# Layer 2 attention: two heads per multiply slot, each in its own 64 array rows, with the row maxima sent to the stacks by DMA

## The reference, cut to what matters

```python
q = (x @ Wq).reshape(b, t, N_HEADS, HEAD_DIM).transpose(0, 2, 1, 3)   # 32 heads of 16
k = (x @ Wk).reshape(b, t, N_KV, HEAD_DIM).transpose(0, 2, 1, 3)      # 8 heads of 16
...
q = _apply_rope(q, cos, sin)
k = _apply_rope(k, cos, sin)
k_h = jnp.repeat(k, GROUP_SIZE, axis=1)
v_h = jnp.repeat(v, GROUP_SIZE, axis=1)
scores = jnp.einsum('bhqd,bhkd->bhqk', q, k_h) / math.sqrt(HEAD_DIM)
scores = jnp.where(causal[None, None], jnp.finfo(scores.dtype).min, scores)
attn = jax.nn.softmax(scores, axis=-1)
ctx = jnp.einsum('bhqk,bhkd->bhqd', attn, v_h)
```

## Time and profile before

| | |
|---|---|
| median of 3 runs | 1157.61 us (1157.04 to 1157.73) |
| the profiled execution | 1157.12 us, with a span of 1155.6 us in the trace |
| busy: PE, PEld | 1124.1 us (97%), 935.9 us (81%) |
| busy: DVE, ACT, POOL | 742.3 us (64%), 649.1 us (56%), 471.3 us (41%) |
| mean granted TensorE clock | 0.997 of full speed |

### The profile page before, as it was taken

How to read it: one execution, slowest core, us unless ns; L and a number is a source line. 1 busy time by engine, 2 the same in 40 slices (tenths; PEclk the granted TensorE clock), 3 DMA queues, 4 the chain that set the end, 5 groups by cost and what they waited for, 6 DMA issues and landing times. The chain is left out here.

```text
span 1155.6 us, 19856 instructions
## 1 busy us (share of the span) xinstructions
PE 1124.1 (97%) x6378; PEld 935.9 (81%) x6378; DVE 742.3 (64%) x2399; ACT 649.1 (56%) x1492; POOL 471.3 (41%) x537
## 2 busy tenths in 40 slices
PE   7899999999999999999999999999999999999997
PEld 6788888888888888888888878888888777776786
DVE  6767776667776666776677782222334778887675
ACT  6656665566765666765666644544212366666524
POOL 4654553345554355544444333333203355354300
PEclk9999999999999999999999999999999999999999
DMA  6011110011110011100100002221200223421001
GB/s 234 19 37 38 37 37 28 23 37 38 37 37 28 22 45 30 46 29 19 37 28 1 28 19 57 81 73 45 66 1 19 63 59 79 127 61 32 2 1 73
DMA packets 30361, 51.20 MB, mean 44 GB/s; under 512 B 5680, under 2 KB 6576, under 8 KB 30256
## 3 DMA queue, kind: packets, MB, share of 16 engines
q1 hardware_dynamic: 29680, 48.85, 14.9%
q10 hardware_dynamic: 576, 1.05, 0.3%
HBM read 38.35 MB, written 2.10 MB: 35 GB/s over the span
## 5 line engine op out<-in xcount | busy, mean ns | idle before, releaser
L487 POOL TENSOR_TENSOR turned<-turned,sin 128x512 f32<-128x512 f32 x73 | 94.4, 1293 | 310.2 <-ACT turned L347 310.2
L1719 DVE CUSTOM_DVE_ANT_0 f_masked<-bank,a_mask 128x512 f32<-128x512 f32 (+3 forms) x256 | 110.0, 486 | 26.2 <-PE bank L1931 21.7
L363 ACT ACTIVATE probs<-probs,neg_max 128x256 f32<-128x256 f32 (+1 forms) x256 | 119.8, 473 | 11.3 <-DVE neg_max L580 11.3
L490 POOL TENSOR_TENSOR turned<-turned,by_cos 128x512 f32<-128x512 f32 x73 | 101.0, 1384 | 5.7
L96 PE MATMUL bank<-wo_hi,oT_hi 128*128 128x512 f32 x256 | 100.3, 392 | 1.6 <-DVE oT_lo L643 1.6
L734 PE MATMUL bank<-xT_hi,wq_hi 128*128 128x512 f32 x256 | 101.7, 397 | 0.0
L734 PE MATMUL bank<-xT_lo,wq_hi 128*128 128x512 f32 x256 | 100.3, 392 | 0.0
L734 PE MATMUL bank<-xT_hi,wq_lo 128*128 128x512 f32 x256 | 100.1, 391 | 0.0
L96 PE MATMUL bank<-wo_hi,oT_lo 128*128 128x512 f32 x256 | 99.9, 390 | 0.0
L96 PE MATMUL bank<-wo_lo,oT_hi 128*128 128x512 f32 x256 | 99.7, 389 | 0.0
L422 ACT ACTIVATE pT_hi<-bank 128x512 fp32r<-128x512 f32 x112 | 61.6, 595 | 52.0 <-PE bank L773 52.0
(11 more groups left out here) (247 smaller groups left out, 3213.5 us busy)
## 6 DMA issues: line engine op xcount, KB each, us to landing
staged<-weights SPq DMA_DIRECT2D x70, 256.0 KB, 2.7
f_staged<-weights_f SPq DMA_DIRECT2D x33, 256.0 KB, 2.7
f_q_stack<-a_qT_hi SPq DMA_DIRECT2D x64, 64.0 KB, 2.0
rows<-x_rows SPq DMA_DIRECT2D x2, 1024.0 KB, 7.2
f_k_stack<-a_kT_hi SPq DMA_DIRECT2D x64, 32.0 KB, 2.0
f_q_stack<-a_qT_lo SPq DMA_DIRECT2D x32, 64.0 KB, 2.0
out<-rows SPq DMA_DIRECT2D x8, 256.0 KB, 2.0
a_raw<-weights_qkv SPq DMA_DIRECT2D x4, 384.0 KB, 4.8
```

Source lines behind the costliest of these rows:

```text
L363: act.activation(probs[:, s % 2, h, 0:width], probs[:, s % 2, h, 0:width], ACT.Exp, bias=neg_max[:, s % 2, h:h + 1], scale=SCALE0, accum_o ...
L487: pool.tensor_tensor(at, at, sin[:, :], ALU.mult).then_inc(sin_done, 1)
L490: pool.tensor_tensor(at, at, by_cos_at(a, first), ALU.add).then_inc(roped, 1)
L1719: dve.tensor_tensor_reduce(masked[:, bank * SEQ + at:bank * SEQ + at + seen], ps_s[bank][:, at:at + seen], mask[:, SEQ - seen:SEQ], -1.0, ...
```

## The change

Keys and queries are laid out anew. Of the 64 rows of one half of the array, row 4d + part holds dimension d of a head's part (high, low, high), so one head's stack fills 64 rows, and two heads of a pair stand in the two halves. Each multiply names only its half's rows; `scores(j, piece)` and `cross(j, piece)` issue the pair's two multiplies of a tile one behind the other, into different banks. Every fourth row of the key stack holds ones; four rows of the query stack take the maxima of the pair. These arrive by DMA: ACT copies the turned maxima of a whole unit (eight rows) to `shift_rows`, and SP sends them on (`load_shift`, two DMAs per unit); since the scores are taken from the same stack before, SP first clears those rows (`clear_shift`).

The heads' pieces are now items: item 6j + 2*piece + n is head n of pair j. Three banks serve all items in turn, for scores and for cross alike, so two items of one piece take two banks. `ps_o` is one bank where it was two, and the eighth bank takes the turned maxima. `apply` has two parts. Keys are turned doubled, in four parts where there were two, so there are twelve turns; two of them (10 and 11) stand at pair 9. Key DMAs carry 32 rows where they carried 16, and there are four query and key stacks.

```diff
@@ -1193,7 +1193,8 @@
-STACK = PARTS * PAIR_ROWS
+HALF = P // 2
+SPREAD = HALF // HD1
...
+ITEMS = 2 * PIECES
 SCORES_AT = {3: (0, 0), 2: (1, 0), 0: (1, 3 * P), 1: (2, 0)}
+SCORE_TILES = ((3,), (2, 0), (1,))
+MAXIMA_AFTER = (1, 2, 4, 6, 7, 8)
+PAIR_MAXIMA = 2 * SEQ_TILES
...
-STACKS = 3
...
+STACKS = 4
...
-APPLY_KEYS = ((0,), (1,), (3, 2))
+APPLY_KEYS = ((0, 3), (1, 2))
...
-PARTS_IN_LOOP = {0: 7, 1: 8, 2: 9}
...
+TURNS = [("q", 0), ("q", 1), ("q", 2), ("q", 3), ("k", 0), ("k", 1), ("q", 4), ("q", 5), ("q", 6), ("q", 7), ("k", 2), ("k", 3)]
...
+PARTS_IN_LOOP = {(0, 2): 8, (1, 1): 9, (9, 1): 10, (9, 2): 11}
...
-        ps_s, ps_t, ps_o = psum[0:3], psum[3:6], psum[6:8]
+        ps_s, ps_t, ps_o, ps_max = psum[0:3], psum[3:6], psum[6], psum[7]
...
+        def before_items(n):
+            return PAIR_MAXIMA * (n // ITEMS) + (MAXIMA_AFTER[n % ITEMS - 1] if n % ITEMS else 0)
...
+                    sp.dma_start(k_stacks[u % STACKS][part::SPREAD, :].bitcast(F32),
...
+            def load_shift(u):
+                sp.wait_ge(max_in, u + 1)
+                for pair in range(2):
+                    sp.dma_start(q_stacks[u % STACKS][SHIFT_STEP - 1::SHIFT_STEP, pair, :].bitcast(F32),
+                                 shift_rows[PAIR_SHIFTS * pair:PAIR_SHIFTS * (pair + 1), u % 2, :].bitcast(F32)
+                                 ).then_inc(shift_in, 16)
...
+            for u in range(STACKS - 1):
+                load_keys(u)
+                load_queries(u, 0)
+                load_queries(u, 1)
+            load_shift(0)
+            for u in range(STACKS - 1, UNITS1):
...
+                if u >= STACKS:
+                    sp.wait_ge(crossed, 2 * ITEMS * (u - STACKS + 1))
+                load_keys(u)
+                if u >= STACKS:
+                    clear_shift(u)
+                load_queries(u, 0)
+                load_shift(u - STACKS + 2)
+                load_queries(u, 1)
...
+                if j == 10:
+                    act.wait_ge(stack_in[(KV1 - 1) % STACK_SEMS][0], keys_in(KV1 - 1))
...
+            pool.memset(shift_places[:, :, :].bitcast(F32), 0.0)
+            for r in range(STACKS):
+                pool.memset(q_stacks[r][:, :, :].bitcast(F32), 0.0)
+                ones_in = pool.memset(k_stacks[r][:, :].bitcast(F32), 1.0)
...
+            def maxima(j, piece):
...
+                for n in range(2):
+                    item = ITEMS * j + 2 * piece + n
+                    dve.wait_ge(scored, item + 1)
+                    for qt in SCORE_TILES[piece]:
...
+                    if j % 2 == 0 and piece == 1 and u >= 2:
+                        join(u - 2)
+                    if j % 2 == 1 and piece == 2 and u >= 1:
+                        evacuate(u - 1)
+                    if j + AHEAD_PAIRS < PAIRS1:
+                        maxima(j + AHEAD_PAIRS, piece)
+            join(UNITS1 - 2)
...
+            def scores(j, piece):
+
+                u, pair = divmod(j, 2)
+                r = u % STACKS
+                if piece == 0:
+                    pe.wait_ge(stack_in[u % STACK_SEMS][pair], keys_in(u) if pair == 0 else 16 * PARTS * (u // STACK_SEMS + 1))
+                items = [ITEMS * j + 2 * piece + n for n in range(2)]
+                if items[1] >= 3:
+                    pe.wait_ge(max_done, before_items(items[1] - 2))
+                for qt in SCORE_TILES[piece]:
+                    at, seen = SCORES_AT[qt][1], (qt + 1) * P
+                    for n, item in enumerate(items):
+                        rows_at = slice(n * HALF, (n + 1) * HALF)
+                        mm = pe.matmul(ps_s[item % 3][:, at:at + seen], q_stacks[r][rows_at, pair, qt * P:(qt + 1) * P],
+                                       k_stacks[r][rows_at, 0:seen], start=True, stop=True, skip_group_check=True)
+                        if qt == SCORE_TILES[piece][-1]:
+                            mm.then_inc(scored, 1)
...
+            def cross(j, piece):
+
+                u, pair = divmod(j, 2)
+                r = u % STACKS
+                if j == 0 and piece == 0:
                     pe.wait_ge(part_lo, PARTS_AFTER[TILES - 2][0] + 1)
+                if pair == 0 and piece == 0:
+                    pe.wait_ge(shift_in, 16 * 2 * (u + 1))
+                items = [ITEMS * j + 2 * piece + n for n in range(2)]
+                if items[1] >= 3:
+                    pe.wait_ge(exp_done, items[1] - 2)
+                for kb in CROSS_KEYS[piece]:
+                    at = CROSS_AT[kb][1]
+                    for n, item in enumerate(items):
+                        rows_at = slice(n * HALF, (n + 1) * HALF)
+                        mm = pe.matmul(ps_t[item % 3][:, at:at + SEQ - kb * P], k_stacks[r][rows_at, kb * P:(kb + 1) * P],
+                                       q_stacks[r][rows_at, pair, kb * P:SEQ], start=True, stop=True, skip_group_check=True)
+                        if kb == CROSS_KEYS[piece][-1]:
+                            mm.then_inc(crossed, 1)
...
-                if u >= 2 and part == 0:
-                    pe.wait_ge(finished, u - 1)
+                if u >= 1 and part == 0:
+                    pe.wait_ge(finished, u)
...
+            scores(0, 2)
+            for piece in range(PIECES):
+                scores(1, piece)
+            scores(2, 0)
             turn_maxima(0)
+            scores(2, 1)
+            scores(2, 2)
+            for piece in range(PIECES):
+                scores(3, piece)
+            for j in range(PAIRS1):
+                u = j // 2
+                for piece in range(PIECES):
+                    cross(j, piece)
+                    if j + AHEAD_PAIRS < PAIRS1:
+                        scores(j + AHEAD_PAIRS, piece)
+                    if j % 2 == 0 and piece == 1 and u + 1 < UNITS1:
+                        turn_maxima(u + 1)
+                    if (j, piece) in PARTS_IN_LOOP:
+                        turn_part(PARTS_IN_LOOP[j, piece])
+                    if u >= 1 and (j % 2, piece) == (0, 2):
+                        apply(u - 1, 0)
+                    if u >= 1 and (j % 2, piece) == (1, 0):
+                        apply(u - 1, 1)
+                    if u >= 1 and (j % 2, piece) == (1, 2):
+                        turn_output(u - 1)
```

More of the change, by code:

```diff
@@ L1296, in attention1 @@
         o_tok = q_tok
[L1297 to L1300 removed]
+        k_stacks = [sb(f"k_stack{r}", [P, SEQ], F32R) for r in range(STACKS)]
         last_pT = sb("last_pT", [P, RING - FIRST_PT, HEAD_PROBS])
@@ L1471, in _ @@
                         sp.dma_start(place[:, :, :], w_f1[some].rearrange("k p c -> p k c")[:, :, 0:D]).then_inc(main_in, 16)
+            for u in range(UNITS1 - STACKS + 2, UNITS1):
+                load_shift(u)
             for tile in range(TILES):
@@ L1617, in turn_rows @@
                 pool.tensor_tensor(q_tok[:, tile, :], by_cos[:, 0:D], by_sin[:, 0:D], ALU.add).then_inc(tok_done, 1)
-                pool.tensor_tensor(k_tok[:, tile, :], by_cos[:, D:], by_sin[:, D:], ALU.add).then_inc(tok_done, 1)
+                turned = k_tok[tile // SEQ_TILES][:, tile % SEQ_TILES, :].rearrange("p (g a d) -> p g a d", a=2, d=HD1)
+                cos_part, sin_part = (by[:, D:].rearrange("p (g a d) -> p g a d", a=1, d=HD1).broadcast_to([P, KV1, 2, HD1])
+                                      for by in (by_cos, by_sin))
+                pool.tensor_tensor(turned, cos_part, sin_part, ALU.add).then_inc(tok_done, 1)
             for tile in range(TILES - 1):
@@ L1747, in _ @@
                     low_part(j)
-            maxima(0)
-            maxima(1)
+            for piece in range(PIECES):
+                maxima(0, piece)
             rotate(TILES - 1)
-            maxima(2)
-            maxima(3)
-            for s in range(SLOTS1 + 1):
-                if s in PARTS_IN_LOOP:
-                    low_part(PARTS_IN_LOOP[s])
-                if s % GROUP1 == 0 and s >= 2 * GROUP1:
-                    join(s // GROUP1 - 2)
-                if s % GROUP1 == 3 and s > GROUP1:
-                    evacuate(s // GROUP1 - 1)
-                if s + AHEAD_SCORES < SLOTS1:
-                    maxima(s + AHEAD_SCORES)
+            for j in range(1, AHEAD_PAIRS):
+                for piece in range(PIECES):
+                    maxima(j, piece)
+            for j in range(PAIRS1):
+                u = j // 2
+                for piece in range(PIECES):
+                    if (j, piece) in PARTS_IN_LOOP:
+                        low_part(PARTS_IN_LOOP[j, piece])
+                    if j % 2 == 0 and piece == 1 and u >= 2:
[5 more added lines that the diff above has]
+            join(UNITS1 - 2)
             steps = [0]
@@ L1908, in turn_part @@
                 else:
-                    pe.wait_ge(tok_done, 2 * (n + 1) * SEQ_TILES)
-                    pieces = [k_tok[:, n * SEQ_TILES + tile, :] for tile in range(SEQ_TILES)]
-                if j == 7:
-                    pe.wait_ge(sin_done, 4 * TILES)
-                elif j >= 8:
+                    b, c = divmod(n, 2)
```

(7 more changed lines are left out.)

271 lines of the change are left out of this document (100 added, 171 removed).

## The result

The changed kernel takes 1201.89 us (median of 4, 1200.94 to 1203.79) against 1157.55: slower by a ratio of 1.0386, 95% interval 1.0368 to 1.0404. I had forecast 1177.5 and a range up to 1196: the direction was right, but of the 44.3 us lost my sum had 20.4, less than half.

What follows compares the result with a forecast made beforehand. PE bound the kernel before, DVE next; after the change, their waits set the pace: 924.4 + 11.3 + 13 x 10.65 + 3.8 + 7.8 + 6.8 = 1092.6, 20.2 later; 20.4 put on 1157.12 gave 1177.5 us, range 1149 to 1196.

Steps and rivals of the forecast that it cites:

- The bound and the way it is reached: In the loop: PE's sum falls to 6.5 to 7 us per unit, under DVE's 7.8, but waits between engines set the pace.
- walk: One loop unit followed wait by wait from its first cross: next unit at 10.44 us, DVE idle 2.6, PE 3.
- My 0.2 on top: Per loop unit: 0.2 us added to the walk, as the kernel before walked 9.62 against 9.84 measured; gives 10.65.
- The clock: Longer start wait and PE's gaps in the loop may bring slow-clock stretches again, about 1 us each; not in the sum.
- The first cross: Way into the loop: first cross at 924.4, where before it was 914.14, behind the scores of four whole pairs.
- DVE's start at 909.1: Ahead of the loop: DVE starts the maxima near 909.1, 0.4 later for four more turnings of the second key part.
- My 1.2 for waits at pieces: Ahead of the first cross: about 1.2 us of DVE's waits at pieces, one term of the 924.2.
- The parts: Parts 10 and 11, at pair 9: two DVE waits for PE's turning and ACT's high part, 3.8 us in all.
- The halves: A pair's multiplies in the array's two row halves run at once, some ns apart; four groups of 0.65 per unit.
- The rival's unit of 11.65 + 0.2: Rival that the halves do not overlap, chance 0.10: loop unit 11.65 + 0.2 us, 19 us more, 1196 in all.
- DVE keeps full: Rival, chance 0.17: PE returns in time, loop unit is DVE's 7.85 us, total 1141; decides at 9.1 per unit.
- SP, POOL and the switches: SP's DMAs 7.6 of 10.65 us per unit and POOL's clearing cost nothing; row-group switches some 0.9 per unit.

Runs made afterwards that it cites:

- full_rows: Changed kernel with every multiply of scores and cross over all 128 rows, pairs serial, both heads summed, exponential of a ten-thousandth: 1201.09 us.
- fill: Changed kernel with three unread 512-column multiplies over all 128 rows added on PE per unit, units 1 to 13 save 4: 1194.94 us.
- copy_early: Changed kernel with DVE's copy of a unit's outputs moved alone, to the second pair's second piece: 1180.12 us.
- own_bank: Changed kernel with the sixth turned part (second key part) given bank 1 for itself: 1198.01 us.
- order: Changed kernel with only places moved: apply in three parts, maxima turned a piece later, DVE's copy and division a piece earlier: 1172.52 us.
- low_later: Changed kernel with scores ten pieces ahead, another order, second key part's own bank, unread multiplies added at the start, low parts a piece later: 1152.76 us.
- one_half: Changed kernel with both heads of a pair multiplying from rows 0 to 63, second head's own keys and queries left out: 1266.90 us.
- best_full_rows: low_later with serial pairs over all 128 rows, both heads summed, exponential of a ten-thousandth: 1163.84 us.

## Why the prediction failed, step by step

- **The bound and the way it is reached.** Right. PE's sum fell and the three shared banks, with PE in order, set the pace: walk 10.44, measured 10.49; DVE's idle time 2.6, measured 2.4; `turn_output`'s wait 1.07, measured 0.91. My 0.2 on top was not needed at full clock (13 x 0.16 = 2.1 too much).
- **The clock.** The step that failed: "may bring such stretches again, about 1 us each". I had named the cause and a price, and put no term in the sum, since I gave it no count. The price was near (0.6 to 2.2 us per unit); the count was twelve of thirteen units. Together that is some 16.5 in units 1 to 13 (what 10.49 and the parts leave), which full_rows confirms (0.9 left there, the clock full) and fill in part (7.0 won while work was added). The 2.7 at the end is the clock's as well: unit 14 took 10.5 with a stretch at 0.50 in it, and 7.7 in fill and 7.8 in copy_early at full clock, the forecast's 7.8. I misread the one row I had, 0.88 behind the loop's start: in the kernel before that is one fall, right behind a thin place (PE busy 1.09 of 2.00 us from 921 to 923), and PE then has no such gap again until the loop's end. The changed kernel has 2.3 us of waits in every unit, so the fall comes back again and again. "No gain can come from it" was right.
- **The first cross.** 931.2, not 924.4. DVE's start at 909.1 was the wrong term, by 4.9: I charged the second key part 0.4 for its turnings and did not look at the bank it goes to. PE's wait of 2.65 and the half clock behind it (0.83 in 895 to 905) made it 913.96; own_bank gave 3.9 back. My 1.2 for waits at pieces was 2.5 (0.47, 0.60, 0.59, 0.60 and 0.28 in DVE's timeline). The rest of the 6.8, under 1, I have not separated.
- **The parts.** 3.8 for parts 10 and 11 was right (3.5), and I left out the same for parts 8 and 9 in unit 0 (2.8). One wait of that kind stood in the earlier trace rows from the very place.
- **The halves.** Right: they overlap. The rival's unit of 11.65 + 0.2 was 11.58 when built (full_rows); its 1196 came out at 1201.1, with the same late first cross (6.7) in it.
- **The rivals.** "DVE keeps full" needed 9.1 per unit. It can be had by order alone (8.81), and with the second key part's bank, the low parts and the start's clock mended as well (low_later) the change then does win. As the change stood, nothing spoke for it.
- **SP, POOL and the switches.** Nothing speaks against what I said. In the loop of low_later (8.84 per unit) PE's multiplies waited 0.8 us in all for POOL, and its loads 0.4 us for the shift rows' DMA. What the switches cost by themselves no run measured; they fit into a unit of 8.81.
- **How the 26.2 add up.** The clock 16.5 + 2.7, the first cross 6.8, the low parts of 8 and 9 in unit 0 2.6, less the 2.1 of my 0.2 and 0.3 on parts 10 and 11. So my too dear unit hid 2.1 of the miss.

The Trainium skill describes a failure of this kind: in TensorE: Matmul & The Clock Gate, section "A second HAM failure mode: psum-queue depth-cycling", a kernel that cycles through PSUM banks has PE idle for short times between groups of multiplies, often enough to make its clock swing between the two levels. The traces here agree: waits of 0.40 to 0.91 us in a unit, and stretches at 0.58 to 0.84 beside one at 1.00. It had belonged among the rivals with a price.

What the clock follows was taken apart only in part. Waits of PE matter: order has the same multiplies in halves with 0.9 us of waits in a unit, where the changed kernel has 2.3, and keeps 1.00 from 1005 on. (fill has 1.3 and full_rows 1.5 in a unit.) The rows matter too: one_half has no gap in whole stretches and is at 0.50, full_rows with the same serial pairs over all rows is at 1.00. fill cannot tell the two, since its added multiplies both shorten the waits and use all rows.

## What to carry to other kernels

When a change takes work off the engine that was never idle, ask first what its new gaps do to its clock, and give that a term with a size. Shorter multiplies won nothing in the order they were given, and about 10 us in another: with shared banks and an engine that takes its program in order, the place of a copy can be worth more than the work saved (21.8 us for one call). Walk one unit with its waits, and then move what the last wait is for. And for every operation that is added ahead of a loop, look up the bank or buffer it goes to and who still reads it.

## What the runs showed of the hardware

- Multiplies whose result nobody reads made the kernel faster (fill, 7.0 us). Three of 512 columns per unit lay wholly in PE's waits, and the granted clock stood at 1.00 from 1003 to 1083, where without them it had fallen again and again.
- The clock fell although no wait of PE between 931 and 1101 of the changed kernel was longer than 2.0 us, and its 47 waits there were 0.66 long on average.
- PE busy 10.00 of 10 us at a granted clock of 0.50 (one_half, rows 0 to 63 only), against 1.00 with PE busy 8.6 when the same serial pairs took all 128 rows (full_rows): 1266.9 against 1201.1. The two differ in the rows named, in the values that follow from that, and in the scale of the exponential; whether rows or values count was not taken apart.
- A pair in two halves of the rows takes 0.50 where the same two in a row over all rows take 0.71 to 0.73, both at full clock (changed kernel, full_rows, best_full_rows).
